# A fused decoder-style kernel on one core: early up weights for the last routed stage, and down weights rounded by a product instead of a cast

## The chip, the cores and the metric
The kernel runs on one core of one Trainium2 chip. Its engines are TensorE (PE for matmuls, PEld for its weight loads), VectorE (DVE), ScalarE (ACT), GpSimd (POOL) and SyncE (SP), which here only issues transfers. Times are device microseconds of one execution, as a median over several. Fewer is better.

## The reference
The program is one layer chain over 2048 tokens of width 256: a dense mixture of eight gated experts and a shared one, an attention with a hyperbolic distance, a typed feed-forward stage, rotary attention with a layer norm and a short convolution in front, and a mixture of four experts, one per token. What the change touches is in the last three.

```python
# typed stage: the expert is given by the sequence's type (8 -> 5 experts)
h = jax.nn.relu(jnp.einsum('bsd,bdf->bsf', x, wi[type_label]))
eo = jnp.einsum('bsf,bfd->bsd', h, wo[type_label])
...
x = x + _attn(x, ln1_w, ln1_b, conv_w, attn_w, proj_w, n_head)      # rotary attention
# last stage: the expert is the router's argmax, known only after attention
h = _layernorm(x, ln_w, ln_b)
expert_idx = jnp.argmax(h @ router_w, axis=-1)
for e in range(E):                                                  # E = 4
    gate_raw, value = jnp.split(h @ expert_wv[e], 2, axis=-1)
    y = gate_raw * jax.nn.sigmoid(gate_raw) * value @ expert_proj[e]
    out = out + jnp.where((expert_idx == e)[..., None], y, 0.0)
```

All is float32. The kernel multiplies in a rounded form (fp32r): each operand is split into a rounded part (`_hi`) and a remainder (`_lo`), and three of the four products are summed.

## The kernel before
Two stages are built by one function, `routed_ffn`: the typed one (tag `typed`, one up matrix per expert, relu) and the last one (tag `moe`, two up matrices, gate and value, silu). Tokens are sorted by expert into 11 **slots** of 256 rows, so that a slot has one expert. Per slot SP loads the expert's up weights (1 MB per matrix) and down weights (1 MB) into one of two stage buffers, POOL gathers the 256 rows from a table in HBM by two indirect transfers (`gather`, line 2144) and later scatters the result by two more (`send`, line 2336).

A slot has eight steps f. In each, PE does the up products of 128 hidden features (`up_step`, line 2380, twelve in moe) and, three steps behind, six down products (`dn_step`, line 2399); after step 1 it transposes the next slot's rows (`turn`, line 2367). ACT rounds the up weights of the next slot (`w_hi`, line 2447), takes silu (line 2463) and rounds the hidden values (`h_hi`, line 2451). POOL subtracts to get `w_lo` (line 2327). DVE makes the gated product (line 2555), `h_lo` (line 2522) for the step before, and every second step a **group** for the down weights: it rounds one piece (`d_hi`, line 2514; ACT rounds the other, line 2457) and makes two `d_lo` (line 2517). In step 3 it makes `x_lo` (line 2507) behind the group, in step 4 it takes the last slot's result. All engines' orders are written out by hand; PE's down product of a step waits for `h_lo` of that step.

The last stage begins with the sort (`SortFirst`). DVE turns the router's choices into places: `count_up`, `bound`, `put` (each token's place), `own` (each slot's expert, for which SP waits), then `row_numbers`, `hot_tokens`, `hot_rows` and `take` (the list of rows, for which POOL waits before it gathers for slots 0 and 1 and only then makes `w_lo` of slot 0). The arrays of the list lie in the second down buffer until PE has `found` the rows. Slot 0 has expert 0 always, so SP loads its weights at once.

The typed stage ends with `LoadLate`: behind the last stage load SP issues the weights of the join and of rotary attention. In rotary attention SP brings each of 16 units by `bring` (line 1395), then `fetch`, `bring_sum`, `bring_x` and `store`, each of another unit, in this order.

Of the kernel before, what the change touches and what calls it, by code (L numbers as in the profile page):

```python
# [692 lines left out]
class Router:  # L693


    def __init__(self, nc, ctx, ln_w, ln_b, w_r, x_rows, table, sel):
        sb = lambda name, shape: ctx.enter_context(nc.sbuf_tensor(f"router_{name}", shape, F32))
        self.x_rows, self.table, self.sel = x_rows, table, sel
# [296 lines left out]
def attention(nc, m, tag, hyper, srcT, resT, w, router=None, stored=None):  # L995
# [14 lines left out]
    with ExitStack() as s:  # L1010
# [329 lines left out]
        with ExitStack() as s2:  # L1340
# [42 lines left out]
            with nc.Block() as block:  # L1383
                @block.sync
                def _(sp):
# [730 lines left out]
class SlotStage:  # L2116
# [6 lines left out]
    def __init__(self, nc, ctx, m, tag, ups, experts, up, down, table, target, sent, stored):  # L2123
# [23 lines left out]
    def load_up(self, sp, e, q):  # L2147
        for j, src in enumerate(self.up_source(e)):
            sp.dma_start(self.up[:, q, j], src).then_inc(self.up_loaded[q], 16)
# [38 lines left out]
class LoadLate(Prelude):  # L2188
# [3 lines left out]
    def __init__(self, *weights):  # L2192
        self.weights = weights

    def sync_late(self, sp):
        for w in self.weights:
            w.load(sp)


class SortFirst(Prelude):  # L2200


    def __init__(self, lists, slots):
        self.lists, self.slots = lists, slots
# [8 lines left out]
    def sync(self, sp):  # L2213
        self.slots.load_slot(sp, 0, 0)
# [3 lines left out]
        sp.wait_ge(self.lists.found, 1)  # L2218
        self.slots.load_down(sp, e, 1)
# [8 lines left out]
    def vector(self, dve):  # L2228
        lists = self.lists
        lists.count_up(dve)  # L2230
        lists.bound(dve)
        lists.put(dve)
        lists.own(dve)
# [5 lines left out]
        self.wait_stored(dve)  # L2239
# [8 lines left out]
def routed_ffn(nc, m, tag, swiglu, stage, prelude):  # L2248
# [20 lines left out]
    with ExitStack() as s_:  # L2269
# [31 lines left out]
        with nc.Block() as block:  # L2301
# [21 lines left out]
            def _(pool):  # L2323
                def up_lo(s, f, q):

                    pool.wait_ge(up_rounded, FC * s + f + 1)
                    pool.tensor_tensor(w_lo[:, :, :, fs(f)], stage_up[:, q, :, :, fs(f)], w_hi[:, :, :, fs(f)],  # L2327
# [105 lines left out]
            def _(act):  # L2433
# [9 lines left out]
                def round_up(s, nth, q, f):  # L2443
# [3 lines left out]
                    act.activation(w_hi[:, :, :, fs(f)], stage_up[:, q, :, :, fs(f)], ACT.Copy).then_inc(up_rounded, 1)  # L2447
# [53 lines left out]
            def _(dve):  # L2501
# [122 lines left out]
def program(nc, a, out):  # L2624

    with ExitStack() as ctx:
# [73 lines left out]
        with ExitStack() as s, ExitStack() as right:  # L2700
# [5 lines left out]
            with ExitStack() as f:  # L2706
# [25 lines left out]
                routed_ffn(nc, m, "typed", False, slots, LoadLate(joining, rope))  # L2732
# [3 lines left out]
            router = Router(nc, s, a["L0_ffn_ln2_w"], a["L0_ffn_ln2_b"], a["L0_ffn_router_w"], typed_table, moe_table, m.moe_sel)  # L2736
# [3 lines left out]
        with ExitStack() as s:  # L2740
            wv = a["L0_ffn_expert_wv"]
            halves = lambda e: tuple(up(wv)(e)[:, :, j * F:(j + 1) * F] for j in range(2))
            slots = SlotStage(nc, s, m, "moe", 2, E_MOE, halves, down(a["L0_ffn_expert_proj"]), moe_table,
                              out.rearrange("b t d -> (b t) d"), [s.enter_context(nc.semaphore(f"moe_sent{i}")) for i in range(2)], moe_stored)
# [3 lines left out]
            routed_ffn(nc, m, "moe", True, slots, SortFirst(lists, slots))  # L2748
# [30 lines left out]
```

## Time and profile before

| | us |
|---|---|
| median of 3 runs | 2192.46 (2191.4 to 2193.07) |
| the profiled execution | 2192.84 |
| its span | 2191.0 |
| PE busy in the span | 2006.2 (92%) |
| DVE, ACT, POOL busy | 1124.4, 910.9, 697.6 |

The span is the time between the first and last instruction; 1.84 us lie around it. PE is busy for most of it, so time can be won only where PE sits idle or runs at a low clock. In the page's 40 slices of 54.8 us PE's busy tenths are 9 nearly everywhere in the first half, and lower around the joins between stages. The last stage covers slices 36 to 40, where PE reads 5, 9, 9, 9, 8, DVE 4, 7, 8, 8, 6 and POOL 6, 8, 8, 8, 5. A 9 can still hide a tenth of the time. Stages are therefore read one by one, by windows and timelines.

### The profile page before, as it was taken

What the parts mean: (1) busy time and instruction counts of PE and PEld (TensorE: products, weight loads), DVE (VectorE), ACT (ScalarE), POOL (GpSimd) and SP (SyncE); (2) the same over time, 40 slices, a digit from 0 to 9 for tenths busy, and PEclk for the clock granted to TensorE, in tenths of its full rate; (3) what the DMA queues carried; (4) which work ended last, traced back from release to release, by engine and by line L of the source; (5) the groups of instructions that cost most, each with busy time, mean ns of one, the idle gap of its engine ahead of it and who ended that gap; (6) DMA issues with size and microseconds to landing.
All of it is one profiled execution on the core that took longest, in us unless ns stands there. A gap on an engine that the chain in (4) does not pass through costs nothing. (4 is left out here: it accounts for less than half of the span.)

```text
span 2191.0 us, 34148 instructions
## 1 busy us (share of the span) xinstructions
PE 2006.2 (92%) x12638; PEld 1697.1 (77%) x12638; DVE 1124.4 (51%) x1964; ACT 910.9 (42%) x1898; POOL 697.6 (32%) x778
## 2 busy tenths in 40 slices
PE   7999999999999999999998767899999766959998
PEld 6888888888888888888887645788799544849997
DVE  3334434434434434433434687442488565847886
ACT  4242332424233242332423579322355354636564
POOL 3030210303012030200300068211298233968885
PEclk9999999999999999999999879899999877979999
DMA  5010010100001010020000300320066113556651
GB/s 166 1 45 14 1 57 0 58 0 30 27 0 57 0 57 0 0 84 0 0 1 0 78 2 3 116 77 10 29 210 215 47 38 117 179 197 199 201 190 55
DMA packets 95631, 140.30 MB, mean 64 GB/s; under 512 B 15310, under 2 KB 72560, under 8 KB 95536
## 3 DMA queue, kind: packets, MB, share of 16 engines
q1 hardware_dynamic: 88480, 123.02, 17.6%
q0 software_dynamic: 4928, 12.86, 1.7%
q10 hardware_dynamic: 2128, 3.15, 0.4%
q8 instruction: 61, 1.00, 0.2%
q14 instruction: 34, 0.28, 0.0%
HBM read 109.37 MB, written 12.06 MB: 55 GB/s over the span
## 5 line engine op out<-in xcount | busy, mean ns | idle before, releaser
L603 DVE TENSOR_TENSOR cond_h<-cond_silu,ps 128x512 f32<-128x512 f32 x288 | 198.1, 688 | 697.5 <-ACT cond_silu L514 694.1
L514 ACT ACTIVATE cond_silu<-ps 128x512 f32<-128x512 f32 x288 | 172.3, 598 | 771.8 <-PE ps L433 771.8
L433 PE MATMUL ps<-a_x_hi,cond_w_hi 128*128 128x512 f32 x1152 | 449.8, 390 | 2.0 <-DVE a_x_lo L265 2.0
L433 PE MATMUL ps<-a_x_lo,cond_w_hi 128*128 128x512 f32 x1152 | 449.2, 390 | 0.0
L433 PE MATMUL ps<-a_x_hi,cond_w_lo 128*128 128x512 f32 x1152 | 449.1, 390 | 0.0
L402 POOL TENSOR_TENSOR cond_w_lo<-cond_stage_up,cond_w_hi 128x256 fp32r<-128x256 f32 x144 | 108.7, 773 | 832.8 <-ACT cond_w_hi L495 832.8
L433 PEld LDWEIGHTS ps<-a_x_hi,cond_w_hi 128*128 128x128 f32 x1152 | 216.9, 188 | 47.4 <-DVE a_x_lo L265 2.4
L433 PEld LDWEIGHTS ps<-a_x_hi,cond_w_lo 128*128 128x128 f32 x1152 | 216.9, 188 | 45.2
L433 PEld LDWEIGHTS ps<-a_x_lo,cond_w_hi 128*128 128x128 f32 x1152 | 217.0, 188 | 45.0
L449 PE MATMUL ps<-cond_h_hi,cond_d_hi 128*128 128x512 f32 x576 | 224.4, 390 | 3.4 <-DVE cond_h_lo L571 3.4
L449 PE MATMUL ps<-cond_h_hi,cond_d_lo 128*128 128x512 f32 x576 | 224.1, 389 | 0.0
L449 PE MATMUL ps<-cond_h_lo,cond_d_hi 128*128 128x512 f32 x576 | 224.1, 389 | 0.0
L571 DVE TENSOR_TENSOR cond_h_lo<-cond_h,cond_h_hi 128x512 fp32r<-128x512 f32 x288 | 199.6, 693 | 0.1
L508 ACT ACTIVATE cond_h_hi<-cond_h 128x512 fp32r<-128x512 f32 x288 | 179.6, 624 | 0.3 <-DVE cond_h L603 0.3
L449 PEld LDWEIGHTS ps<-cond_h_hi,cond_d_hi 128*128 128x128 f32 x576 | 108.1, 188 | 27.4 <-issue 2.2
L2327 POOL TENSOR_TENSOR moe_w_lo<-moe_stage_up,moe_w_hi 128x512 fp32r<-128x512 f32 x88 | 115.3, 1336 | 33.5 <-ACT moe_w_hi L2447 33.2
L449 PEld LDWEIGHTS ps<-cond_h_hi,cond_d_lo 128*128 128x128 f32 x576 | 108.1, 188 | 22.5
L449 PEld LDWEIGHTS ps<-cond_h_lo,cond_d_hi 128*128 128x128 f32 x576 | 108.1, 188 | 22.3
L574 DVE SCALAR_TENSOR_TENSOR dense_h_lo<-ps,dense_h_hi 128x512 fp32r<-128x512 f32 x64 | 44.3, 692 | 116.5 <-ACT dense_h_hi L520 116.4
L2380 PE MATMUL ps<-moe_x_hi,moe_w_hi 128*128 128x256 f32 x352 | 100.6, 286 | 1.4 <-DVE moe_x_lo L2507 1.4
L2380 PE MATMUL ps<-moe_x_lo,moe_w_hi 128*128 128x256 f32 x352 | 100.4, 285 | 0.0
L2380 PE MATMUL ps<-moe_x_hi,moe_w_lo 128*128 128x256 f32 x352 | 100.3, 285 | 0.0
(378 smaller groups left out, 4019.9 us busy)
## 6 DMA issues: line engine op xcount, KB each, us to landing
moe_stage_up<-in_L_ffn_expert_wv SPq DMA_DIRECT2D x22, 1024.0 KB, 9.2
typed_stage_up<-in_L_cond_wi SPq DMA_DIRECT2D x11, 1024.0 KB, 5.0
typed_stage_dn<-in_L_cond_wo SPq DMA_DIRECT2D x11, 1024.0 KB
moe_stage_dn<-in_L_ffn_expert_proj SPq DMA_DIRECT2D x11, 1024.0 KB, 5.4
cond_stage_up<-in_L_cond_Wg SPq DMA_DIRECT2D x7, 1024.0 KB, 5.0
cond_stage_up<-in_L_cond_Wu SPq DMA_DIRECT2D x7, 1024.0 KB, 7.1
cond_stage_dn<-in_L_cond_Wd SPq DMA_DIRECT2D x7, 1024.0 KB, 5.5
rope_v_now<-rope_v_blk SPq DMA_DIRECT2D x16, 272.0 KB, 2.4
```

What stands on the lines that cost most here:

```text
L402: ins = pool.tensor_tensor(w_lo[:, j, :, c], stage_up[:, j, :, c], w_hi[:, j, :, c], ALU.subtract)
L433: ins = pe.matmul(up_ps[st % 2][j], w[:, j, k, fs], x[:, k, tok], start=(i == 0), stop=(i == 3 * KC - 1))
L449: ins = pe.matmul(y_ps[tt % 2][c], w[:, f, cs], x[:, st % HB], start=(f == 0 and i == 0), stop=(f == FC - 1 and i == 2))
L508: act.activation(h_hi[:, st % HB], h[:, st % 2], ACT.Copy).then_inc(h_rounded, 1)
L514: act.activation(silu[:, st % 2], up_ps[st % 2][0], ACT.Silu).then_inc(act_done, 1)
L571: dve.tensor_tensor(h_lo[:, st % HB], h[:, st % 2], h_hi[:, st % HB], ALU.subtract).then_inc(h_ready, 1)
L574: dve.scalar_tensor_tensor(h_lo[:, st % HB], up_ps[st % 2][0], 0.0, h_hi[:, st % HB], ALU.max, ALU.subtract).then_inc(h_ready, 1)
L603: dve.tensor_tensor(h[:, st % 2], silu[:, st % 2], up_ps[st % 2][1], ALU.mult).then_inc(up_free, 1)
L2327: pool.tensor_tensor(w_lo[:, :, :, fs(f)], stage_up[:, q, :, :, fs(f)], w_hi[:, :, :, fs(f)], ALU.subtract).then_inc(up_ready, 1)
L2380: ins = pe.matmul(up_ps[f % UB][j], w[:, j, k, fs(f)], x[:, q, k], start=(i == 0), stop=(i == 3 * KC - 1))
```

## The change
1. Rounding: in `round_dn` of both routed stages DVE no longer copies a piece of the down weights into the rounded type; it multiplies it by a column of ones.
2. The up weights of the last stage's slot 0 are loaded in eight pieces of 256 KB into the memory of `xT`, which is free by then. SP issues one behind each `bring` of units 2 to 9.
3. At the start of the last stage SP loads down 0 first, then, after `owned`, up 1, and down 1 only after `found` and after slot 0's gather has landed.
4. `own` stands ahead of `put`, and DVE waits for the table's stores before `row_numbers` and no longer at the end.
5. `LoadLate` waits for the landing of the last slot's gather before it issues the late weights.

```diff
@@ bring, in rotary attention @@
                         sp.dma_start(x[:, q], qk[:, bass.ds(i, 1)].rearrange("p o n -> p (o n)")).then_inc(brought[q], 16)
+                        if isinstance(i, int):
+                            router.first_up.load(sp, i - 2)
@@ SlotStage @@
-        self.up, self.down = sb("stage_up", [P, 2, ups, KC, F]), sb("stage_dn", [P, 2, FC, D])
+        self.up = [sb("stage_up0", [P, ups, KC, F]) if first_up is None else first_up, sb("stage_up1", [P, ups, KC, F])]
+        self.down = sb("stage_dn", [P, 2, FC, D])
@@ new @@
+class FirstUp:
+    def __init__(self, nc, ctx, room, sources):
+        self.loaded = ctx.enter_context(nc.semaphore("moe_first_up_loaded"))
+        self.up = room.rearrange("p (j k f) -> p j k f", j=len(sources), k=KC)
+        self.pieces = [(self.up[:, j, k, c], src[:, k, c]) for j, src in enumerate(sources) for k in range(KC)
+                       for c in (slice(0, F // 2), slice(F // 2, F))]
+
+    def load(self, sp, n):
+        if 0 <= n < len(self.pieces):
+            dst, src = self.pieces[n]
+            sp.dma_start(dst, src).then_inc(self.loaded, 16)
@@ LoadLate @@
     def sync_late(self, sp):
+        sp.wait_ge(self.slots.x_loaded[(SLOTS - 1) % 2], 16 * (SLOT // P) * ((SLOTS + 1) // 2))
         for w in self.weights:
             w.load(sp)
@@ SortFirst @@
     def sync(self, sp):
-        self.slots.load_slot(sp, 0, 0)
+        self.slots.load_down(sp, 0, 0)
+        sp.wait_ge(self.first_up.loaded, 16 * len(self.first_up.pieces))
+        sp.nop().then_inc(self.slots.up_loaded[0], 16 * self.slots.ups)
         sp.wait_ge(self.lists.owned, 1)
         e = self.slots.expert(sp, 1)
         self.slots.load_up(sp, e, 1)
         sp.wait_ge(self.lists.found, 1)
+        sp.wait_ge(self.slots.x_loaded[0], 16 * (SLOT // P))
         self.slots.load_down(sp, e, 1)
...
+        lists.own(dve)
         lists.put(dve)
-        lists.own(dve)
+        self.wait_stored(dve)
         lists.row_numbers(dve)
...
-        self.wait_stored(dve)
@@ round_dn, DVE @@
-                        dve.tensor_copy(d_hi[:, f], stage_dn[:, q, f]).then_inc(dn_rounded[1], 1)
+                        one = m.const[:, C_ONE:C_ONE + 1].to_broadcast([P, D])
+                        dve.tensor_tensor(d_hi[:, f], stage_dn[:, q, f], one, ALU.mult).then_inc(dn_rounded[1], 1)
```

Three places show what moves. First SP's order at the start of the last stage, before (`moe_stage_up` and `moe_stage_dn` are the stage buffers):

```order
L2302 UNCONDITIONAL_BRANCH
L2149 DMA moe_stage_up<-in_L_ffn_expert_wv 128x2x1024 x2
L2152 DMA moe_stage_dn<-in_L_ffn_expert_proj 128x8x256
L2136 TENSOR_LOAD slot_expert
L2136 ISA x2
L2149 ISA
L2149 DMA moe_stage_up<-in_L_ffn_expert_wv 128x2x1024
L2149 ISA
L2149 DMA moe_stage_up<-in_L_ffn_expert_wv 128x2x1024
L2152 ISA
L2152 DMA moe_stage_dn<-in_L_ffn_expert_proj 128x8x256
```

and now:

```order
L2325 UNCONDITIONAL_BRANCH
L2155 DMA moe_stage_dn<-in_L_ffn_expert_proj 128x8x256
L2139 TENSOR_LOAD slot_expert
L2139 ISA x2
L2152 ISA
L2152 DMA moe_stage_up<-in_L_ffn_expert_wv 128x2x1024
L2152 ISA
L2152 DMA moe_stage_up<-in_L_ffn_expert_wv 128x2x1024
L2155 ISA
L2155 DMA moe_stage_dn<-in_L_ffn_expert_proj 128x8x256
```

The two up loads of slot 0 are gone from here, the down load stands first, and the rest keeps its order.

Second DVE's order in the sort, from the end of `bound` on, before (`moe_past`, `moe_owner` and `slot_expert` are `own`, `moe_place` and `moe_at` are `put`):

```order
L2047 TENSOR_TENSOR moe_start<-moe_end,moe_used 128x4
L2053 TENSOR_TENSOR moe_place<-moe_sums,ps 128x64
L2054 TENSOR_TENSOR moe_place<-moe_place,ps 128x64
L2055 TENSOR_TENSOR moe_place<-moe_place,moe_start 128x64
L2056 TENSOR_TENSOR moe_place<-moe_place,moe_sel 128x64
L2057 TENSOR_REDUCE moe_at<-moe_place 128x16
L2063 TENSOR_TENSOR moe_past<-const,moe_end 128x44
L2065 TENSOR_REDUCE moe_owner<-moe_past 128x11
L2066 TENSOR_SCALAR slot_expert<-moe_owner 128x11
L2071 TENSOR_TENSOR moe_stage_dn<-moe_at,const 128x368
```

and now:

```order
L2049 TENSOR_TENSOR moe_start<-moe_end,moe_used 128x4
L2065 TENSOR_TENSOR moe_past<-const,moe_end 128x44
L2067 TENSOR_REDUCE moe_owner<-moe_past 128x11
L2068 TENSOR_SCALAR slot_expert<-moe_owner 128x11
L2055 TENSOR_TENSOR moe_place<-moe_sums,ps 128x64
L2056 TENSOR_TENSOR moe_place<-moe_place,ps 128x64
L2057 TENSOR_TENSOR moe_place<-moe_place,moe_start 128x64
L2058 TENSOR_TENSOR moe_place<-moe_place,moe_sel 128x64
L2059 TENSOR_REDUCE moe_at<-moe_place 128x16
L2073 TENSOR_TENSOR moe_stage_dn<-moe_at,const 128x368
```

`own`'s three instructions moved ahead of `put`'s five.

Third a group of the down weights on DVE in a moe slot, with what follows it, before:

```order
L2514 CAST moe_d_hi<-moe_stage_dn 128x256
L2517 TENSOR_TENSOR moe_d_lo<-moe_stage_dn,moe_d_hi 128x256 x2
L2555 TENSOR_TENSOR ps<-moe_silu,ps 128x256
L2522 TENSOR_TENSOR moe_h_lo<-ps,moe_h_hi 128x256
L2555 TENSOR_TENSOR ps<-moe_silu,ps 128x256
L2522 TENSOR_TENSOR moe_h_lo<-ps,moe_h_hi 128x256
L2514 CAST moe_d_hi<-moe_stage_dn 128x256
```

and now:

```order
L2538 TENSOR_TENSOR moe_d_hi<-moe_stage_dn,const 128x256
L2541 TENSOR_TENSOR moe_d_lo<-moe_stage_dn,moe_d_hi 128x256 x2
L2579 TENSOR_TENSOR ps<-moe_silu,ps 128x256
L2546 TENSOR_TENSOR moe_h_lo<-ps,moe_h_hi 128x256
L2579 TENSOR_TENSOR ps<-moe_silu,ps 128x256
L2546 TENSOR_TENSOR moe_h_lo<-ps,moe_h_hi 128x256
L2538 TENSOR_TENSOR moe_d_hi<-moe_stage_dn,const 128x256
```

The order is the same; the cast became a product of two tensors.

## Rows read from the trace of the kernel before
**Rows 1.** Windows, all engines; columns: PE, PEld, DVE, ACT, POOL busy us, clock, DMA, GB/s.
```profile
1640.00:1652.00 12.00, 12.00 (x103) 12.00 (x102) 11.10 (x22) 7.19 (x21) 11.30 (x17) 1.00 0.65 218
...
2050.50:2070.00 19.50, 17.98 (x150) 17.77 (x149) 17.08 (x30) 11.77 (x30) 15.63 (x17) 1.00 0.60 196
```

**Rows 2.** Timeline of PE, moe stage; columns: start, us, engine, line, operation, idle before.
```profile
1977.02 0.60 PE L2367 MATMUL ps<-const,moe_x_row 128*128 128x128 f32 x4
...
1995.23 0.60 PE L2367 MATMUL ps<-const,moe_x_row 128*128 128x128 f32 x4
...
2012.94 0.60 PE L2367 MATMUL ps<-const,moe_x_row 128*128 128x128 f32 x4
...
2024.49 0.39 PE L2399 MATMUL ps<-moe_d_hi,moe_h_hi 128*128 128x256 f32 x1 [0.16 <-DVE moe_h_lo L2522]
...
2063.44 0.39 PE L2399 MATMUL ps<-moe_d_hi,moe_h_hi 128*128 128x256 f32 x1 [1.52 <-DVE moe_h_lo L2522]
...
2147.90 0.60 PE L2367 MATMUL ps<-const,moe_x_row 128*128 128x128 f32 x4
```

**Rows 3.** Timeline of DVE, the down-weight group of step 3 in two moe slots.
```profile
2018.98 2.42 DVE L2514 CAST moe_d_hi<-moe_stage_dn 128x256 fp32r<-128x256 f32 x1
...
2021.33 1.85 DVE L2517 TENSOR_TENSOR moe_d_lo<-moe_stage_dn,moe_d_hi 128x256 fp32r<-128x256 f32 x2
...
2056.56 4.89 DVE L2514 CAST moe_d_hi<-moe_stage_dn 128x256 fp32r<-128x256 f32 x1
```

**Rows 4.** Timeline of POOL over the same step of the second slot.
```profile
2056.22 5.07 POOL L2327 TENSOR_TENSOR moe_w_lo<-moe_stage_up,moe_w_hi 128x512 fp32r<-128x512 f32 x4
```

**Rows 5.** Groups by form on DVE, typed then moe: busy us, mean ns, idle before.
```profile
L2514 DVE CAST typed_d_hi<-typed_stage_dn 128x256 fp32r<-128x256 f32 x44 | 20.9, 476 | 0.0
...
L2517 DVE TENSOR_TENSOR typed_d_lo<-typed_stage_dn,typed_d_hi 128x256 fp32r<-128x256 f32 x88 | 55.1, 665 | 0.9 <-ACT typed_d_hi L2457 0.9
...
L2524 DVE SCALAR_TENSOR_TENSOR typed_h_lo<-ps,typed_h_hi 128x256 fp32r<-128x256 f32 x88 | 35.8, 416 | 22.1 <-ACT typed_h_hi L2469 21.2
...
L2514 DVE CAST moe_d_hi<-moe_stage_dn 128x256 fp32r<-128x256 f32 x41 | 64.7, 1577 | 0.0
...
L2517 DVE TENSOR_TENSOR moe_d_lo<-moe_stage_dn,moe_d_hi 128x256 fp32r<-128x256 f32 x80 | 37.6, 509 | 0.0
```

**Rows 6.** Line 2517 (d_lo), both stages: duration ns min/median/max.
```profile
L2517 DVE TENSOR_TENSOR typed_d_lo<-typed_stage_dn,typed_d_hi x88: 406/418/2209, 1577.3 to 1707.2; 128x256 fp32r<-128x256 f32 x88
...
L2517 DVE TENSOR_TENSOR moe_d_lo<-moe_stage_dn,moe_d_hi x88: 408/411/1543, 1964.5 to 2172.5; 128x256 fp32r<-128x256 f32 x88
```

**Rows 7.** Start of the moe stage: timeline rows, the second is the gather's issue.
```profile
1956.46 0.94 SPq L2149 DMA_DIRECT2D moe_stage_up<-in_L_ffn_expert_wv  x2
...
1963.50 0.99 POOL L2144 DMA_INDIRECT moe_x_row<-moe_table,slot_source  x1 [0.15 <-issue]
...
1967.52 11.15 POOL L2327 TENSOR_TENSOR moe_w_lo<-moe_stage_up,moe_w_hi 128x512 fp32r<-128x512 f32 x9
...
1969.82 0.72 PEld L2367 LDWEIGHTS ps<-const,moe_x_row 128*128 128x128 f32 x4 [8.98 <-DMA moe_x_row<-moe_table,slot_source]
...
1972.35 0.58 PE L2380 MATMUL ps<-moe_x_hi,moe_w_hi 128*128 128x256 f32 x1 [1.41 <-DVE moe_x_lo L2507]
```

**Rows 8.** Line 2144 (gathers), from issue to landing: whole trace, then 1665 to 1669.
```profile
DMA to landing us min/median/max: 2.7/6.3/9.5
...
DMA to landing us min/median/max: 4.3/5.2/6.1
```

**Rows 9.** Timeline at the end of the typed stage.
```profile
1680.14 2.51 SPq L1751 DMA_DIRECT2D join_g<-in_L_cond_g  x2
...
1689.28 0.94 PE L2367 MATMUL ps<-const,typed_x_row 128*128 128x128 f32 x4 [2.96 <-DMA typed_x_row<-typed_table,slot_source]
...
1692.80 0.34 PE L2399 MATMUL ps<-typed_d_hi,typed_h_lo 128*128 128x256 f32 x1
```

**Rows 10.** Waits in rotary attention: engine and line, releaser, us, times, longest.
```profile
POOL router_rows L1712 <- DMA moe_table<-router_rows: 0.4, 1, 0.4
```

More of the change, by code:

```diff
@@ L2116, with __init__ @@
 class SlotStage:
-    def __init__(self, nc, ctx, m, tag, ups, experts, up, down, table, target, sent, stored):
+    def __init__(self, nc, ctx, m, tag, ups, experts, up, down, table, target, sent, stored, first_up=None):
         sb = lambda name, shape: ctx.enter_context(nc.sbuf_tensor(f"{tag}_{name}", shape, F32))
@@ L2190, with __init__ @@
     rows_first = True
-    def __init__(self, *weights):
-        self.weights = weights
+    def __init__(self, slots, *weights):
+        self.slots, self.weights = slots, weights
     def sync_late(self, sp):
+        sp.wait_ge(self.slots.x_loaded[(SLOTS - 1) % 2], 16 * (SLOT // P) * ((SLOTS + 1) // 2))
         for w in self.weights:
@@ L2200, with __init__ @@
 class SortFirst(Prelude):
-    def __init__(self, lists, slots):
-        self.lists, self.slots = lists, slots
+    def __init__(self, lists, slots, first_up):
+        self.lists, self.slots, self.first_up = lists, slots, first_up
     def wait_stored(self, eng):
@@ L2326, in up_lo @@
                     pool.wait_ge(up_rounded, FC * s + f + 1)
-                    pool.tensor_tensor(w_lo[:, :, :, fs(f)], stage_up[:, q, :, :, fs(f)], w_hi[:, :, :, fs(f)],
+                    pool.tensor_tensor(w_lo[:, :, :, fs(f)], stage_up[q][:, :, :, fs(f)], w_hi[:, :, :, fs(f)],
                                        ALU.subtract).then_inc(up_ready, 1)
@@ L2446, in round_up @@
                         act.wait_ge(up_loaded[q], 16 * ups * (nth + 1))
-                    act.activation(w_hi[:, :, :, fs(f)], stage_up[:, q, :, :, fs(f)], ACT.Copy).then_inc(up_rounded, 1)
+                    act.activation(w_hi[:, :, :, fs(f)], stage_up[q][:, :, :, fs(f)], ACT.Copy).then_inc(up_rounded, 1)
                 def round_hidden(s, f):
@@ L2731, in program @@
                                       a["L0_ffn_conv_w"])
-                routed_ffn(nc, m, "typed", False, slots, LoadLate(joining, rope))
+                routed_ffn(nc, m, "typed", False, slots, LoadLate(slots, joining, rope))
             join(nc, m, m.typed_rows, sent, m.sumT, s0, s1, joining, rope)
@@ L2735, in program @@
             second.close()
-            router = Router(nc, s, a["L0_ffn_ln2_w"], a["L0_ffn_ln2_b"], a["L0_ffn_router_w"], typed_table, moe_table, m.moe_sel)
+            wv = a["L0_ffn_expert_wv"]
+            halves = lambda e: tuple(up(wv)(e)[:, :, j * F:(j + 1) * F] for j in range(2))
+            first_up = FirstUp(nc, ctx, m.xT.rearrange("p c n -> p (c n)"), halves(0))
+            router = Router(nc, s, a["L0_ffn_ln2_w"], a["L0_ffn_ln2_b"], a["L0_ffn_router_w"], typed_table, moe_table, m.moe_sel,
+                            first_up)
             attention(nc, m, "rope", False, s0, m.sumT, rope, router, moe_stored)
         with ExitStack() as s:
-            wv = a["L0_ffn_expert_wv"]
-            halves = lambda e: tuple(up(wv)(e)[:, :, j * F:(j + 1) * F] for j in range(2))
             slots = SlotStage(nc, s, m, "moe", 2, E_MOE, halves, down(a["L0_ffn_expert_proj"]), moe_table,
-                              out.rearrange("b t d -> (b t) d"), [s.enter_context(nc.semaphore(f"moe_sent{i}")) for i in range(2)], moe_stored)
+                              out.rearrange("b t d -> (b t) d"), [s.enter_context(nc.semaphore(f"moe_sent{i}")) for i in range(2)], moe_stored, first_up.up)
             sem = StageSemaphores(nc, "moe_sort")
@@ L2747, in program @@
                           m.moe_sel, E_MOE, m.bank[0:2], slots.down[:, 1].rearrange("p f d -> p (f d)"), True)
-            routed_ffn(nc, m, "moe", True, slots, SortFirst(lists, slots))
+            routed_ffn(nc, m, "moe", True, slots, SortFirst(lists, slots, first_up))
             sem.give_back()
```

6 lines of the change are left out of this document (3 added, 3 removed).

## The prediction
> **What bounds the kernel now.** I read the page first, then the waits and the timeline of each stage. The change touches the two routed stages (typed, 1573 to 1718 us, and moe, from 1950 us) and the rotary attention between them; everything before is left alone. One word for what follows: a slot is 256 rows through one expert, 11 per stage, and each runs eight steps, in which TensorE (PE) does up and down products, VectorE (DVE) makes the down weights' parts and h_lo, GpSimd (POOL) makes w_lo.
>
> In a typed slot PE is busy for all of 12.0 us, with DVE at 11.1 and POOL at 11.3 close behind; in a late moe slot of 19.5 us PE is busy for 17.98 only [rows 1]. One moe slot shows no idle: from transposes to transposes 1995.23 to 2012.94, 17.71 us, at the full clock. That is PE's own pace. In the slot from 2050.5 PE instead waits 1.52 us for h_lo at 2063.44 [rows 2]. DVE's timeline says why: the CAST that rounds down weights began at 2056.56 and took 4.89 us, where typed casts of the same shape average 0.48 [rows 5]; it ended 0.2 us after POOL's run of four w_lo (2056.22 plus 5.07) [rows 3, 4]. DVE stands still while POOL runs from one instruction into the next. The 41 casts of this stretch average 1577 ns, and the d_lo behind them, two SBUF inputs each, 509 [rows 5]. So the moe stage is bound by PE plus one stall by CAST per slot.
>
> The price of all stalls, by PE's own pace: between the first and the last transposes (1977.02 and 2147.90, nine slots) lie 170.9 us [rows 2]. Eight slots of 17.71 and the first, which lacks twelve down products of 0.12 us (a slot's 17.71 over its 148 PE instructions; 16.27), are 157.95. The rest is 12.9 us, and the last slot's two short waits add about 0.9: **13.8 us**.
>
> The stage's start: the second gather of slot 0 is issued at 1963.50 and lands at 1969.8, 6.3 us later, and the first up product comes at 1972.35, 2.5 us behind (transposes, x_hi, x_lo). Five MB of weights are in flight by then, the second 2 MB from 1956.46 [rows 7]. The best gather of the whole trace took 2.7 us, and typed ones beside 2 MB of weights 4.3 to 6.1 [rows 8].
>
> The typed stage's end: PE waits 2.96 us at 1689.28 for the last slot's gather, which took the 9.5 us of the whole trace's maximum; behind it on the queues lay the join's weights, issued by SP from 1680.14 [rows 8, 9].
>
> **The change part by part, against the profiled run (2192.84 us; its median is 0.4 lower).**
>
> (1) Up weights early. Eight pieces of 256 KB go out behind brings 2 to 9 of rope_x, and 2 MB disappear from the moe stage's start. Down 0 goes first there; up 1 goes out sooner than 1956.46, since own (three operations) now stands ahead of put's five; down 1 (1 MB) waits for slot 0's gather. When the gathers go out, only the rest of up 1 is in flight. I take 3.2 us for the landing (2.7 is the floor, 4.3 the typed figure beside a full load), which is 1966.7 instead of 1969.8. The next limit is close: POOL does four gathers first and starts w_lo(0,0) only at 1967.52 [rows 7], done at 1968.8, so the first product can't come before 1968.9, and by my landing comes at 1969.3. **Gain 3.0** (0 to 3.4). What is queued behind SP's new wait: down 1, then up 2 and down 2. Down 1 is due at step 4 of slot 0, four steps of at least 1.4 us after 1969.3 with two more at half speed, not before 1976; at the worst typed figure of 6.1 us [rows 8] it lands at 1973. Up 2 waited for POOL's eighth w_lo before (eight ninths of 11.15 us after 1967.52, about 1977.4) and still does. ScalarE's w_hi no longer waits for a load, but nobody waits for w_hi before POOL is free: worth nothing by itself. The moved wait for the table's rows is over when it is reached.
>
> (2) The pieces in rotary attention. Each costs SP about half a microsecond (0.94 for two in [rows 7]); SP then waits for PE anyway before the next fetch, and the fetches behind may find 256 KB on the queues. The only waits on a transfer there, after the first one, are 0.4 us by POOL [rows 10], so transfers have slack and this work hides them; if it did not, eight times 0.5 would be 4. **Loss 0.3** (0 to 4).
>
> (3) The product with one. It takes the cast's place 44 times in each routed stage. The nearest row is d_lo: same shape, same type, two SBUF inputs: 0.41 us alone, at most 1.54 in moe, that is one w_lo passed and no more, though runs of four w_lo occurred [rows 6]. So I expect: a product gets in between two w_lo, where the cast waited for the end of the run. But then both d_lo behind it meet POOL again. The group of step 3 takes 4.89 us and two d_lo of 0.41 now (about 5.5 with their overlap) [rows 3, 6] and becomes at most 1.3 + 1.5 + 1.5 = 4.3. How much may it take? The slot with CAST 2.42 and d_lo 1.85 (4.1 together) stalled PE by 0.16 [rows 2, 3], so 3.9 is free and 4.3 stalls by 0.4. With 0.04 for the restart that is 0.45 us on nine slots, 4.0 in all. **Gain in moe 13.8 - 4.0 = 9.8** (0 to 13.8). POOL has 15.6 us of work per slot [rows 1]; each DVE operation that gets in between costs it at most that operation's 0.41, so five more make 17.7, PE's own pace: no cushion is left, but POOL works a slot ahead.
>
> The Trainium skill (SBUF — State Buffer, Who interferes with whom) speaks against this edit: a cast in a 2-port mode and a `tensor_tensor` with both inputs in SBUF both contend with a GpSimd instruction that reads SBUF, and the loser is blocked for the whole instruction. It knows no difference between the two in how many instructions they let pass; by it the gain of this part would be about nil. The trace disagrees, 4.89 us against at most 1.54.
>
> (4) The typed stage. Its casts average 476 ns and its d_lo 665 [rows 5]: the product costs 0.19 us more, 0.8 per slot, where DVE's idle time before h_lo, 22.1 us less the 5.2 of the late gather, is 1.7 us per slot. It fits mostly; POOL gets a little later, and its gathers with it. Against that the join's and rope's weights now wait for the last gather: at 6.1 us [rows 8] it lands at 1685.8, and PE wanted it at 1686.2. That frees the 3.1 us of wait, and some 1.4 us of half speed behind it (from the transposes at 1689.28 to 1692.80, 3.5 us, lie work of four transposes and fourteen products, 2.1 us at 0.12 each). The held loads are due only in the join, whose work waits for the end of this stage anyway. 4.5 less 1.5 for the product and the later POOL: **gain 3.0** (-3 to 4.5).
>
> Sum: 3.0 - 0.3 + 9.8 + 3.0 = 15.5; 2192.84 - 15.5 = **2177 us**.
>
> **The rivals.**
> A, all stalls go: DVE's groups fall where POOL gathers or sends instead of running w_lo. For it: the trace's slot without any idle. 3.0 + 13.8 + 4.5 gives 2171.5. Chance 0.12.
> B, the product waits as long as the cast, because DVE stays locked out through a run of w_lo in step 3 (this is also where the rule named above leads). For it: one typed d_lo took 2.21 us, two w_lo [rows 6]. Only 3.0 + 3.0 - 0.3 are left: 2187. Chance 0.13.
> C, the gather isn't faster for being alone, or POOL is late for another reason, so the early weights do nothing: 2180. Chance 0.07.
> D, slower: the product makes DVE the bound of the typed stage. Its idle time there allows 0.42 more per product, so it decides from a mean of 0.90 us. If half of the products took the 2.21 us of the longest d_lo and half the mean, 1.44, a slot would lose 0.54 x 4 = 2.2 us, ten slots 22, and in moe nothing would be won: -3.0 - 4.5 + 22 = +14.5, that is 2207. Against it: 88 d_lo average 0.665. Chance 0.08.
>
> **How the numbers follow.** The forecast has 0.58, with 2173 to 2182 as its own spread; 0.02 is left over. The range 2171 to 2187 leaves out D and some of B. A measurement of this kernel tells about 0.2% (4.4 us) from no change, so faster means below 2188: forecast, A, C and two thirds of B, 0.85; same 0.06; slower 0.09.
>
> **What would show it.** In moe: d_hi on DVE with a mean near 1.0 us and none above 1.6; slots of 17.7 to 18.3 us; waits of PE for h_lo of 0 to 0.6 each. First up product near 1969.3 less what was won earlier, 7.4 us after the first gather's issue (10.3 before). Typed slots still 11.95, PE's wait for the last gather below 1 us. I am wrong if the product's mean in moe is over 1.5, if typed slots grow past 12.2, or if POOL, not DVE, is what PE waits for.

## The result, and the profile of the changed kernel

The changed kernel takes **2199.19 us** (2198.22 to 2200.5), the kernel before 2192.29 us (2191.4 to 2194.59) beside it: a ratio of 1.0032, with an interval of 1.0022 to 1.0041. It is slower by 7 us, where the forecast was 2177 and 15.5 faster. The profiled run has a span of 2196.7 us, against 2191.0 before.

The line of each stage that answers to [rows 5] and [rows 6] comes first. Groups of the page of after; the columns are line, engine, operation, output from inputs, shapes and count, then busy us and the mean in ns, idle time before them:

```profile
L2538 DVE TENSOR_TENSOR moe_d_hi<-moe_stage_dn,const 128x256 fp32r<-128x256 f32 x44 | 70.8, 1610 | 0.0
L2541 DVE TENSOR_TENSOR typed_d_lo<-typed_stage_dn,typed_d_hi 128x256 fp32r<-128x256 f32 x88 | 55.8, 673 | 0.6 <-ACT typed_d_hi L2480 0.6
L2541 DVE TENSOR_TENSOR moe_d_lo<-moe_stage_dn,moe_d_hi 128x256 fp32r<-128x256 f32 x88 | 49.5, 601 | 0.0
L2538 DVE TENSOR_TENSOR typed_d_hi<-typed_stage_dn,const 128x256 fp32r<-128x256 f32 x44 | 27.6, 627 | 0.0
```

The product with one averages 1610 ns in the moe stage, where the forecast said about 1.0 us. The same line's durations, smallest, median and largest in ns:

```profile
L2538 DVE TENSOR_TENSOR typed_d_hi<-typed_stage_dn,const x44: 407/438/1314, 1575.4 to 1707.9; 128x256 fp32r<-128x256 f32 x44
L2538 DVE TENSOR_TENSOR moe_d_hi<-moe_stage_dn,const x44: 406/1088/5945, 1962.9 to 2177.6; 128x256 fp32r<-128x256 f32 x44
```

"None above 1.6" was the forecast; the longest took 5.9 us. The timeline of DVE (first two rows) and of POOL (third row) in a late moe slot of after, start and duration in us, answers to [rows 3, 4]:

```profile
2060.91 4.70 DVE L2538 TENSOR_TENSOR moe_d_hi<-moe_stage_dn,const 128x256 fp32r<-128x256 f32 x1
2065.53 0.75 DVE L2541 TENSOR_TENSOR moe_d_lo<-moe_stage_dn,moe_d_hi 128x256 fp32r<-128x256 f32 x2
2060.26 5.06 POOL L2350 TENSOR_TENSOR moe_w_lo<-moe_stage_up,moe_w_hi 128x512 fp32r<-128x512 f32 x4
```

POOL's run of four w_lo ends at 2065.32, the product 0.29 us later. It is the picture of [rows 3, 4] with another instruction in it: the product waits for the end of the whole run, as the cast did. The two d_lo behind it take 0.75 together, because the run is over by then. The waits of PE from 1975 to 2190 us (in total, times, longest), before and then after:

```profile
PE ps L2399 <- DVE moe_h_lo L2522: 11.4, 9, 1.7
```
```profile
PE ps L2422 <- DVE moe_h_lo L2546: 13.2, 11, 3.8
```

So no stall is gone, and one has grown to 3.8 us, where the longest was 1.7. It belongs to the first slot. The start of the moe stage in after, on PE and POOL; the first row is the last step of the sort, which hands the gathers their lists:

```profile
1960.10 0.33 PE L2102 MATMUL ps<-moe_token_hot,moe_stage_dn 128*128 128x44 bf16 x4 [7.88 <-DVE moe_stage_dn L2094]
...
1965.20 0.99 POOL L2147 DMA_INDIRECT moe_x_row<-moe_table,slot_source  x1 [0.15 <-issue]
...
1968.93 9.93 POOL L2350 TENSOR_TENSOR moe_w_lo<-xT,moe_w_hi 128x512 fp32r<-128x512 f32 x8
1978.82 1.29 POOL L2350 TENSOR_TENSOR moe_w_lo<-moe_stage_up,moe_w_hi 128x512 fp32r<-128x512 f32 x1
...
1982.95 5.02 POOL L2350 TENSOR_TENSOR moe_w_lo<-moe_stage_up,moe_w_hi 128x512 fp32r<-128x512 f32 x4
```
```profile
1971.04 0.58 PE L2403 MATMUL ps<-moe_x_hi,moe_w_hi 128*128 128x256 f32 x1 [1.41 <-DVE moe_x_lo L2530]
...
1990.34 0.36 PE L2422 MATMUL ps<-moe_d_hi,moe_h_hi 128*128 128x256 f32 x1 [3.77 <-DVE moe_h_lo L2546]
```

The gather of slot 0 (issued 1965.20) was there when PE took it at 1968.51, 3.3 us later, where it was 6.3 before [rows 7]. But the slot that follows took 22.05 us from transposes to transposes, against 18.21 before [rows 2]. The longer wait is only 2.05 us of these 3.84. Windows behind the wait, after and then before (PE, PEld, DVE, ACT, POOL busy us, then clock, DMA, GB/s), show most of the rest:

```profile
1991.00:1993.00 2.00, 2.00 (x11) 2.00 (x11) 2.00 (x3) 1.69 (x5) 1.87 (x2) 0.50 0.99 331
```
```profile
1991.00:1993.00 2.00, 2.00 (x19) 2.00 (x18) 2.00 (x7) 1.33 (x4) 1.81 (x2) 1.00 0.56 193
```

After the wait of 3.77 us PE's granted clock was 0.50, the lower of its two levels (1.2 GHz), and 2 us hold 11 of its products; after the wait of 1.72 us before it stayed at 1.00 (2.4 GHz), with 19. The 18 products from 1990.34 took 3.73 us, where they take 2.2 at the full clock.

The typed stage's third turn. Before, all of DVE's d_lo took at most 2.2 us here [rows 6]; in after one pair reads, with POOL's run and PE's wait beside it:

```profile
1606.83 0.41 DVE L2538 TENSOR_TENSOR typed_d_hi<-typed_stage_dn,const 128x256 fp32r<-128x256 f32 x1
1607.16 5.22 DVE L2541 TENSOR_TENSOR typed_d_lo<-typed_stage_dn,typed_d_hi 128x256 fp32r<-128x256 f32 x2
...
1607.69 4.41 POOL L2350 TENSOR_TENSOR typed_w_lo<-typed_stage_up,typed_w_hi 128x256 fp32r<-128x256 f32 x6
...
1613.37 0.39 PE L2422 MATMUL ps<-typed_d_hi,typed_h_hi 128*128 128x256 f32 x1 [1.57 <-DVE typed_h_lo L2548]
```

A d_lo now met a run of six typed w_lo and waited 5.2 us with its neighbour. At the stage's end PE still waited for the last gather, 2.79 us at 1692.08 (before 2.96 us at 1689.28 [rows 9]), 2.8 us later than before.

The balance of the profiled runs, after less before, in stretches of PE's timeline: to the last typed transposes +2.8; from there to the end of the sort -1.5 (268.02 us for 269.55); from the sort to the first up product -2.6 (10.94 for 13.52); from there to the end of the span +7.0 (225.7 for 218.7). That is +5.7, the difference of the spans. The first two parts are not effects to a microsecond: two later kernels whose code is that of the kernel before up to the last stage (the wait in the kernel before, and the product in moe alone) ended their sort at 1954.98 and 1956.39 us, 3.9 and 2.4 us sooner than the kernel before itself.

### The profile page after: what moved, and what is told of

Same layout as the page of the kernel before. It is cut to its first block and busy times, and to the rows that moved or that the text cites. A ratio compares the mean times of both kernels' runs of the same rounds, so it can differ in the third digit from the quotient of the medians.

```text
span 2196.7 us, 34155 instructions
## 1 busy us (share of the span) xinstructions
PE 2008.3 (91%) x12638; PEld 1697.4 (77%) x12638; DVE 1144.6 (52%) x1964; ACT 910.1 (41%) x1898; POOL 700.8 (32%) x778
## 3 DMA queue, kind: packets, MB, share of 16 engines
q1 hardware_dynamic: 89088, 123.02, 17.7%
## 5 line engine op out<-in xcount | busy, mean ns | idle before, releaser
L2350 POOL TENSOR_TENSOR typed_w_lo<-typed_stage_up,typed_w_hi 128x256 fp32r<-128x256 f32 x88 | 70.3, 827 | 84.9 <-ACT typed_w_hi L2470 84.6
```

Source lines behind the costliest of these rows:

```text
L2350: pool.tensor_tensor(w_lo[:, :, :, fs(f)], stage_up[q][:, :, :, fs(f)], w_hi[:, :, :, fs(f)], ALU.subtract).then_inc(up_ready, 1)
```

## Experiments

Theory T: the product waits like the cast and costs more besides; GpSimd's back-to-back runs of w_lo are what stalls PE. The rivals are named with each run. Every kernel was timed several times beside the kernel before.

### What the product alone does

```diff
-                        one = m.const[:, C_ONE:C_ONE + 1].to_broadcast([P, D])
-                        dve.tensor_tensor(d_hi[:, f], stage_dn[:, q, f], one, ALU.mult).then_inc(dn_rounded[1], 1)
+                        dve.tensor_copy(d_hi[:, f], stage_dn[:, q, f]).then_inc(dn_rounded[1], 1)
```

> The changed kernel with the old cast in place of the product with one, and nothing else. Theory T (the product waits through a whole run of GpSimd's w_lo as the cast did, and the operations behind it got slower, so the product is worth nothing or less; the rest of the change is worth about nothing either): the mean of the cast in the last stage is again about 1.58 us, the typed slots lose their stall of 1.6 us at 1613 and their d_lo of 4.3 us, and the time is 2190 to 2196 us, 3 to 9 below the changed kernel. Rival R (the loss is the early start's, which moves the transfers and the gathers against the down weights' rounding, and the product is a gain beside it): the first slot of the last stage keeps its 22 us, and the time is 2199 to 2206. Rival N (the kinds are equal): 2198 to 2200.

Measured: 2191.57 us, ratio to the kernel before 0.9997 (0.9988 to 1.0006). The reverse edit, in the kernel before:

> The kernel before with the product with one in place of the cast, and nothing else. T: the typed slots get the 0.15 us more that each product takes than a cast on an engine that has only 0.9 us of 12 free, and a stall or two, the slots of the last stage stay at 19.5 to 19.7 us; 2194 to 2201 us, 2 to 9 above the kernel before. R: the slots of the last stage come down, 2182 to 2190 us. N: 2192 within 1.

Measured: 2201.32 us, ratio 1.0040 (1.0026 to 1.0054), just above T's range. So the product costs 7.7 us in the one setting (1.0032 less 0.9997, of 2191.6) and 8.8 in the other, and all that is left of the change, the early weights, the held loads and the new order of the sort, is worth nothing that can be measured. R is out: the product is a gain nowhere. The first slot, though, took 21.8 us with the cast too, so that loss is the early start's own.

Which stage pays was asked with the product in one stage of the kernel before (below the typed stage; the other has `if swiglu`):

```diff
+                        one = m.const[:, C_ONE:C_ONE + 1].to_broadcast([P, D])
+                        if not swiglu:
+                            dve.tensor_tensor(d_hi[:, f], stage_dn[:, q, f], one, ALU.mult).then_inc(dn_rounded[1], 1)
+                        else:
                         dve.tensor_copy(d_hi[:, f], stage_dn[:, q, f]).then_inc(dn_rounded[1], 1)
```

> The kernel before with the product with one in the typed stage alone. From the trace of the kernel before with the product in both stages (its last typed gather's turn comes 3.8 us later, counted from the first turn), T expects 3 to 5 us above the kernel before, by one PE stall of 1.6 us at the third turn, where a d_lo waits through a run of six w_lo, and by later gathers at the end. Rival R (the product costs only in the last stage): within 1 us of the kernel before.

> The kernel before with the product with one in the last stage alone. T: the product waits as the cast did, takes 0.14 us more by itself, and the d_lo behind it take 0.1 us more each (1.4 us of VectorE's time a slot); slots at 19.7 instead of 19.5 us and two dearer first slots; 4 to 6 us above the kernel before, and with the typed stage's share the 9.7 us of both. Rival R (the last stage alone would gain, and only the later end of the typed stage hides it): 2 us or more below the kernel before.

Measured: typed 2194.3 us, ratio 1.0010 (1.0001 to 1.0019); moe 2196.24 us, ratio 1.0023 (1.0014 to 1.0032), beside 2191.35 of the kernel before. That is 2.2 and 5.0 us by the ratios, 7.2 together for the 8.8 of both. The typed figure is below T's 3 to 5, with an interval of 0.2 to 4.2 us. Its trace says more: from the first typed turn to the tenth it took 103.9 us against 100.8 before, 103.6 in the changed kernel and 100.5 in that kernel with the cast. It shows the same stall of 1.6 us at the third turn, and 3.2 us of wait for the last gather. In the moe run the second and third slots took 39.45 us together (35.83 before), and the later ones 19.68 each (19.47).

### Is it the form of the rounding?

ScalarE rounds all eight blocks, DVE only subtracts:

```diff
+                    act.activation(d_hi[:, f], stage_dn[:, q, f], ACT.Copy).then_inc(dn_rounded[f % 2], 1)
...
-                        dve.tensor_tensor(d_hi[:, f], stage_dn[:, q, f], one, ALU.mult).then_inc(dn_rounded[1], 1)
```

> The changed kernel with all eight blocks of the down weights rounded by ScalarE, and no product or cast on VectorE. Each costs ScalarE 0.42 us (the last stage's mean of its own four), so 1.7 us more a slot for an engine that is busy some 14 of 19.7. T (the stall is VectorE's wait behind GpSimd's run, whatever the form of the rounding): VectorE's wait of 1.1 us a time at four places a slot goes, the PE stalls of 1.3 us a slot go, the slots of the last stage come to 18.2 to 18.6 us; 2183 to 2190 us. Rival S (another instruction of VectorE then takes the wait, d_lo first, whose two inputs lie in SBUF too): the means of d_lo rise from 0.62 to 1.0 us or more, slots stay at 19.3 to 19.7, 2193 to 2199. Rival W (VectorE now waits for ScalarE's rounding at the odd blocks, and the chain of the hidden values gets longer): above 2200.

Measured: 2191.54 us, ratio 0.9997 (0.9988 to 1.0006). T's price failed (2183 to 2190), and rival S was right in its picture, though its time of 2193 to 2199 was too high. The group of d_lo in the page of this kernel, and one pair of it with POOL's run beside it:

```profile
L2536 DVE TENSOR_TENSOR moe_d_lo<-moe_stage_dn,moe_d_hi 128x256 fp32r<-128x256 f32 x88 | 98.2, 1143 | 1.1 <-ACT moe_d_hi L2480 1.0
```
```profile
2058.05 5.57 DVE L2536 TENSOR_TENSOR moe_d_lo<-moe_stage_dn,moe_d_hi 128x256 fp32r<-128x256 f32 x2
...
2057.93 5.07 POOL L2350 TENSOR_TENSOR moe_w_lo<-moe_stage_up,moe_w_hi 128x512 fp32r<-128x512 f32 x4
```

With 44 fewer instructions on DVE, their time only falls from the 107.7 us of the kernel with the cast (cast 66.7, d_lo 41.0) to 98.2, and d_lo, whose mean was 0.5 us before [rows 5], is now 1.14. Whichever of the three comes first to this run of four behind the gathers waits for its end. The short d_lo of the moe stage in [rows 6] were short because a cast had waited in front of them.

### Cutting the run

If the run itself is the cause, a pause in it must take the stalls away. One wait does that, in the changed kernel with the cast put back, ahead of the second w_lo of the run:

```diff
                         if not is_last(s):
+                            if swiglu and f == 2:
+                                pool.wait_ge(dn_ready, FC * s + 3 + DN + 1)
                             up_lo(s + 1, f, 1 - q)
```

> The changed kernel with the cast, and with one wait more: in the last stage GpSimd makes the third w_lo of a slot (the second of its run of four behind the gathers) only when VectorE has finished its pair of d_lo at step 3. So the run of four is cut in two and VectorE's cast gets in between. T (VectorE waits through the whole back-to-back run, and that wait is what stalls PE): the cast at that place falls from 4.86 us to 2.3 or less, the PE stalls behind h_lo go, the slots of the last stage come from 19.2 to 19.5 us down to 17.8 to 18.4 us, the first of them from 21.8 to 18.5 us or less; 2174 to 2181 us. Rival P (GpSimd, with 15.6 of 19.5 us busy, is made to idle and becomes the bound): slots at 18.8 to 19.5, 2186 to 2193 us. Rival Q (the cast waits for something else than the run): the cast stays at 4 us or more, 2190 to 2195.

Measured: **2175.39 us**, ratio 0.9935 (0.9922 to 0.9947). POOL and then DVE at that place:

```profile
2046.95 1.31 POOL L2350 TENSOR_TENSOR moe_w_lo<-moe_stage_up,moe_w_hi 128x512 fp32r<-128x512 f32 x1
2049.53 5.13 POOL L2350 TENSOR_TENSOR moe_w_lo<-moe_stage_up,moe_w_hi 128x512 fp32r<-128x512 f32 x4 [1.27 <-DVE moe_d_lo L2542]
```
```profile
2048.50 0.28 DVE L2539 CAST moe_d_hi<-moe_stage_dn 128x256 fp32r<-128x256 f32 x1
2048.69 0.76 DVE L2542 TENSOR_TENSOR moe_d_lo<-moe_stage_dn,moe_d_hi 128x256 fp32r<-128x256 f32 x2
```

POOL stands 1.27 us, the cast takes 0.28 us instead of 4.9, and the run then passes beside x_lo, the products and y_row, which it does not hold (0.69, 0.43, 0.68 us). PE's waits from 1965 to 2180 us, and the windows of one whole slot (PE, PEld, DVE, ACT, POOL busy us, then clock, DMA, GB/s):

```profile
PE ps L2405 <- DVE moe_x_lo L2532: 1.4, 1, 1.4
PE ps L2424 <- DVE moe_h_lo L2547: 0.4, 1, 0.4
PE ps L2432 <- DVE moe_h_lo L2547: 0.3, 1, 0.3
```
```profile
2042.40:2060.10 17.70, 17.70 (x150) 17.70 (x150) 12.40 (x30) 11.67 (x30) 15.26 (x17) 1.00 0.66 220
```

The slot is 17.7 us, all of it PE, and DVE's busy time is 12.4 us instead of the 17.1 of [rows 1]: 4.7 us of that had been waiting. Against the kernel with the cast alone this is 0.0062 of 2191.6, or 13.6 us (12.9 for the same wait in the kernel before, below); the prediction had worked out 13.8 for all the stalls. P and Q are out.

The same wait in the two other settings, and one w_lo earlier (`f == 1`):

> The kernel before with that same wait and nothing else, so that the run of four is cut while the first weights come as they did. T: slots as in the kernel with the cast and the wait, and the start of the last stage as before; the early start then is worth what its first product gained, 2 to 3 us, since the end of GpSimd's run no longer sets the first slot: 2 to 3 us above it, 2177 to 2183 us. Rival E (the early weights are worth nothing even so, since GpSimd's chain of w_lo from the gathers on sets the first slot either way): within 0.7 us of it.

> The changed kernel as it is, with the product with one, and with that same wait. T (the product is dearer by itself, 0.41 us against the cast's 0.27 where nothing is in its way, and lets GpSimd in ahead of the two d_lo behind it; in the typed slots, with 0.9 us of VectorE's 12 free, this costs 3 to 4 us whatever happens in the last stage): 3 to 6 us above the kernel with the cast and the wait. Rival R (the product's cost is one of the runs in the last stage): within 1 us of it.

> As the kernel with the cast and the wait, but the wait stands one w_lo earlier, directly behind the gathers, so that the whole run of four comes after VectorE's pair. T: the cast at that place falls to 1.3 us or less, GpSimd idles some 1.7 us more a slot of the 3.8 it has; the slots are the same as with the wait one later, since no stall of PE is left to take: within 1.5 us of it. Rival P: GpSimd's idle time is used up, w_lo comes late for PE and the time is 2 us or more above it. If it is 2 us or more below it, the gather itself or the first w_lo still held the cast.

Measured, with the kernel before at 2190.24 us beside all four:

| kernel | us | ratio to before | interval |
|---|---|---|---|
| early weights, cast, wait | 2175.39 | 0.9935 | 0.9922 to 0.9947 |
| before, cast, wait | 2177.09 | 0.9941 | 0.9929 to 0.9953 |
| as changed, product, wait | 2179.61 | 0.9952 | 0.9939 to 0.9964 |
| early weights, cast, wait one earlier | 2174.89 | 0.9933 | 0.9921 to 0.9944 |

The early weights show 1.7 us with the run cut, by medians, between rival E's 0.7 at most and T's 2 to 3; the intervals overlap, so this is not settled by time alone. The traces say where it comes from: from the sort's end to the third transposes 33.2 us with them and 35.2 without. The product costs 4.2 us even with the run cut (3.7 by the ratios): T's 3 to 6. Its typed stall of 1.5 us is still there, and its moe mean is 0.97 us beside the cast's 0.57. The wait one w_lo earlier changes nothing more, as expected, since PE had nothing left to wait for.

### What is enough of a pause?

In the changed kernel with the cast, a tiny instruction ahead of each w_lo at steps 2, 3 and 4, with no wait (`tiny` is a tile of its own, with a column for each):

```diff
+                            if swiglu and f in (2, 3, 4):
+                                one = m.const[:, C_ONE:C_ONE + 1]
+                                pool.tensor_tensor(tiny[:, 3 * s + f - 2:3 * s + f - 1], one, one, ALU.mult)
                             up_lo(s + 1, f, 1 - q)
```

> The changed kernel with the cast, and in the last stage one tiny instruction of GpSimd (a product of one column of 128 x 1, about 0.2 us) ahead of the second, third and fourth w_lo of the run of four, with no wait. T1 (VectorE gets in only where GpSimd really stands still, since a tiny instruction of GpSimd keeps the run going): the cast at that place stays at 4.8 us or grows to 5.5, and the time is 2191 to 2195. T2 (any change of instruction, or the pause between them, is enough to let VectorE in): the cast falls to 2 us or less at that place and the time is 2175 to 2181.

Measured: 2193.82 us, ratio 1.0009 (1.0000 to 1.0018). POOL's timeline, and DVE's cast beside it:

```profile
2077.14 1.30 POOL L2351 TENSOR_TENSOR moe_w_lo<-xT,moe_w_hi 128x512 fp32r<-128x512 f32 x1
2078.40 0.20 POOL L2371 TENSOR_TENSOR moe_tiny<-const 128x1 f32<-128x1 f32 x1
2078.55 1.29 POOL L2351 TENSOR_TENSOR moe_w_lo<-xT,moe_w_hi 128x512 fp32r<-128x512 f32 x1
...
2081.34 1.28 POOL L2351 TENSOR_TENSOR moe_w_lo<-xT,moe_w_hi 128x512 fp32r<-128x512 f32 x1
```
```profile
2077.49 5.29 DVE L2541 CAST moe_d_hi<-moe_stage_dn 128x256 fp32r<-128x256 f32 x1
```

T1: the cast sits through four w_lo and three tiny instructions. In one slot of this kernel it got in after two (2.37 us at 2059.41). The kernel before has such a slot without any tiny instruction (the cast of 2.42 us in [rows 3]), so a boundary can let it in, but at this run it seldom does.

The last run starts from the kernel with the cast and the wait one earlier, and puts slot 0's eight w_lo into POOL's idle time ahead of the gathers, beside the sort on DVE:

```diff
-                prelude.gpsimd(pool)
+                if not swiglu:
+                    prelude.gpsimd(pool)
                 for f in range(FC):
                     up_lo(0, f, 0)
+                if swiglu:
+                    prelude.gpsimd(pool)
```

> As the kernel with the cast and the wait directly behind the gathers, but GpSimd makes the eight w_lo of slot 0 ahead of its gathers: the first up weights are there, its w_hi are ready from 1947 to 1951 us on, and it idles 18 us until the sort has its lists. T (whoever reads two SBUF tiles on VectorE waits through the whole run, whatever its form): the sort's small operations, which run at that time, are held up by up to the run's 10 us, the first gather comes 4 to 9 us later, and the shorter first slot gives back about 1; 2178 to 2183 us. Rival M (small operations slip in between two w_lo, or use so little that the run hardly holds them): the first gather comes at most 2 us later, the first slot falls below 17.2 us; 2172.5 to 2176 us.

Measured: 2181.27 us, ratio 0.9953 (0.9940 to 0.9967), by the ratios 4.4 us above the kernel that it was made from. The sort ends at 1963.87 instead of 1955.76, and the first slot falls to 16.3 us. T's time held, but not its picture. DVE's small operations beside POOL's run, which starts at 1948.58:

```profile
1948.64 1.24 DVE L2031 COPY moe_sums<-moe_sums 128x8 f32<-128x8 f32 x1
1949.79 0.20 DVE L2032 TENSOR_TENSOR moe_sums<-moe_sums 128x56 f32<-128x56 f32 x1
1950.03 1.12 DVE L2031 COPY moe_sums<-moe_sums 128x16 f32<-128x16 f32 x1
1951.07 0.20 DVE L2032 TENSOR_TENSOR moe_sums<-moe_sums 128x48 f32<-128x48 f32 x1
1951.30 1.13 DVE L2031 COPY moe_sums<-moe_sums 128x32 f32<-128x32 f32 x1
```

Here an operation waits for one w_lo and gets in, the next one passes freely, and the third waits again. So small operations do pass between two w_lo.

Large ones do too, elsewhere. A typed slot of the kernel before, DVE and POOL, and then a late moe slot of the kernel with the product and the wait:

```profile
1658.29 1.84 DVE L2517 TENSOR_TENSOR typed_d_lo<-typed_stage_dn,typed_d_hi 128x256 fp32r<-128x256 f32 x2
...
1656.75 4.67 POOL L2327 TENSOR_TENSOR typed_w_lo<-typed_stage_up,typed_w_hi 128x256 fp32r<-128x256 f32 x6
```
```profile
2056.80 1.44 DVE L2540 TENSOR_TENSOR moe_d_hi<-moe_stage_dn,const 128x256 fp32r<-128x256 f32 x1
...
2054.13 6.71 POOL L2350 TENSOR_TENSOR moe_w_lo<-moe_stage_up,moe_w_hi 128x512 fp32r<-128x512 f32 x5 [1.04 <-DVE moe_d_lo L2543]
```

Each typed d_lo waits for the w_lo that is running (0.96 us in all) and gets in behind it, with two or three of the run still to come; the product at 2056.80 does the same in a run of five. Counted in the trace of the kernel before, 27 casts and d_lo of the typed stage began inside a run with three or more w_lo left, and 26 of them let at most one end before them, none the whole run. In its moe stage it was 9, of which 7 waited to the end. **What decides stays open.** The sizes of the two instructions do not: the product of 128 x 256 beside w_lo of 128 x 512 does both. No run here separates what is left, such as when the request comes.

### The held loads

```diff
     def sync_late(self, sp):
-        sp.wait_ge(self.slots.x_loaded[(SLOTS - 1) % 2], 16 * (SLOT // P) * ((SLOTS + 1) // 2))
         for w in self.weights:
             w.load(sp)
```

> The changed kernel without the wait that holds the weights of the join and of the rotary attention back until the last typed gather has landed. T (that wait neither gained nor lost, since PE still waits 2.8 us for the last gather): within 1 us of the changed kernel, 2198 to 2200. Rival L (it gained the 1.5 us by which join and attention came closer, or delays the loads that join needs): 2201 to 2204 for a gain undone, 2194 to 2197 for a cost undone.

Measured: 2199.77 us, ratio 1.0034 (1.0022 to 1.0046), the changed kernel's own within its interval. The rows that tell why, in after, on SP, POOL and PE:

```profile
1680.89 0.38 SPq L2152 DMA_DIRECT2D typed_stage_up<-in_L_cond_wi  x1
1682.59 0.37 SPq L2155 DMA_DIRECT2D typed_stage_dn<-in_L_cond_wo  x1
1692.05 0.97 SPq L1753 DMA_DIRECT2D join_g<-in_L_cond_g  x2
```
```profile
1683.11 0.99 POOL L2147 DMA_INDIRECT typed_x_row<-typed_table,slot_source  x1 [0.15 <-issue]
```
```profile
1692.08 0.66 PE L2390 MATMUL ps<-const,typed_x_row 128*128 128x128 f32 x4 [2.79 <-DMA typed_x_row<-typed_table,slot_source]
```

The join's weights do leave later, at 1692.05. The gather was still on its way for 9.0 us (1683.11 to 1692.08), against 9.8 without the wait and 9.5 before. But the two kernels named under the balance, which issue the late weights as before, took 8.5 and 7.9, and the changed kernel with the cast, with the wait in place, 8.8: no gain from the wait can be read from this. Two megabyte loads of the last slot's own weights go out 2.2 and 0.5 us ahead of it, and those are not held. That these are what it waits for was not tried.

## Where the prediction went wrong, step by step

**The bound of the kernel** was read rightly: PE plus DVE's stall behind POOL's run, 13.8 us in all. Cutting the run gave 13.6 us (12.9 in the kernel before), and slots of 17.7. The waits of 1.5 us that PE shows are not the whole price of a stall: a late slot of 19.47 us is 1.76 above 17.71, 0.25 more than its wait. The 0.04 us for a restart in (3) is shown by no run.

**(3), the product with one, is the step that failed.** That the product gets in between two w_lo was concluded from d_lo, of the same shape and with two SBUF inputs, which had never waited more than 1.54 us in moe [rows 6]. But at the run that stalls PE each d_lo stands directly behind a cast that has just waited for the run's end; the rows that looked like evidence were chosen by the very wait in question. With ScalarE rounding, d_lo comes first and takes 5.6 us with its pair. What was foreseen does happen in other runs of w_lo, as shown above, but not at this one. Instead of +9.8 in moe the product brought -5.0 there, and -2.2 in the typed stage (single runs; -7.7 for both in the changed kernel). Two of the prediction's own signs of being wrong came true: the product's mean in moe was 1.61 us, and typed slots grew past 12.2. Part of it is plain length: the product takes 0.41 us with nothing in its way (smallest 406 ns) where the cast takes 0.28. The Trainium skill (SBUF — State Buffer, Who interferes with whom) puts both forms, the cast in a 2-port mode and the `tensor_tensor` with two inputs in SBUF, among those that contend with GpSimd. The prediction had set that aside, and the runs agree with the Trainium skill on it: rival B, 2187, was the right mechanism, and even it left out the product's own cost. The wording of the Trainium skill there, that the other is blocked for the whole instruction, is too mild for this trace, where 4.7 to 5.9 us went by over four instructions.

**(1), the early weights.** The mechanics came true: the gather took 3.3 us (3.2 forecast) and the first up product came 7.5 us after the first gather's issue (7.4 forecast). The term, 3.0, was 2.6 at that product and nothing at the end. It left out that the first slot's end is set by POOL, whose 9 w_lo, gathers and 4 w_lo start after the same gathers as before: from the sort's last step to the end of the run of four lie 27.9 us (1960.10 to 1987.97), and 27.6 before. PE started sooner and waited longer, 3.8 us instead of 1.7, and then ran 18 products at half the clock, some 1.6 us more. With the cast this slot was the same (3.7 us of wait, 21.8 in all), so the product is not the cause. Only with the run cut do the traces keep 2.0 us of the early start.

**(2), the pieces in attention**: 0.3 forecast; no loss is seen. The stretch from the last typed transposes to the sort's end became 1.5 us shorter, which is within what two executions differ by.

**(4), the typed stage**: +3.0 forecast, of which the held loads were 4.5. They gained nothing that can be seen: the times with and without them don't differ, and the gather took 9.0 us where 6.1 was forecast. The 1.5 us put down for the product were in truth the 2.2 us of its single run, in part through a typed d_lo of 4.3 us that no typed row had shown: that slot took 13.78 us and two late ones 12.49 and 12.37, where all had been 11.95; the two slots behind the long one stayed at 11.95 as forecast. Rival D had named the typed stage as the place of a loss, but with DVE as its bound, which it did not become.

The sum by what the runs showed is 0 (early weights and held loads) and -7.7 (product), against the measured -7.

## What to carry to other kernels

Ask of every duration in a trace what ran just before it: an instruction that always follows a waiting one shows its own length and never the wait. Where VectorE and GpSimd both work on SBUF, reckon with a wait as long as GpSimd's back-to-back run, whatever the form of VectorE's instruction, and look in the trace at which runs it happens. Order the two engines there with one wait, so that the run falls beside work on PSUM; here that alone was worth 13 to 14 us, and another rounding instruction nothing or less. A transfer brought forward helps only if no other engine's chain starts from the same event.

## What the hardware showed that I had not expected

- VectorE can be held over several GpSimd instructions: 4.86 us through four w_lo, 5.29 us through four w_lo and three tiny ones, 5.22 us for a typed pair beside a run of six. It need not be: typed d_lo of the same shape got in after one w_lo (0.96 us each) in the middle of runs of six and seven.
- The hold can begin ahead of the run: the product at 1982.32 in after took 5.95 us though POOL's run started at 1982.95, behind an indirect DMA issued at 1981.96.
- Small VectorE operations (128 x 8 to 128 x 56) beside the same w_lo wait for one of them only, 1.1 to 1.2 us, and the next one mostly passes freely (0.2 us).
- TensorE's granted clock was 0.50 for some 3 us behind a wait of 3.77 us and stayed at 1.00 behind one of 1.72, in the same slot of the two kernels.
- The rounding cast of 128 x 256 takes 0.28 us, a product of that shape 0.41.
